# Two-layer graph network with a node update behind it: x + h and its moments formed in the second update, and one power and one row load per tile in the last stage

## What is computed

```python
h = jnp.maximum(_layernorm(x, axis=-1), 0.0)
x = x + _L0_gnn_ref(h, edge_index, ...)       # 2 attention layers, each followed by a node update
h = jnp.maximum(_layernorm(x, axis=-1), 0.0)
x = x + _L1_gnn_ref(h, edge_index, edge_attr_128, ...)

# inside the layers of _L0_gnn_ref, after the attention sum agg:
h = h + agg.reshape(n, TD) @ wo[l] + bo[l]
xn2 = _layernorm(h, ln2_g[l], ln2_b[l])
h = h + jax.nn.gelu(xn2 @ w1[l] + b1[l], approximate=False) @ w2[l] + b2[l]

# inside _L1_gnn_ref:
sum3d = jax.ops.segment_sum(edge_attr @ W_sum + b_sum, src)
cent_term = jax.nn.sigmoid(centralities @ W_cent + b_cent)
vor_term = jax.nn.sigmoid(voronoi_values @ W_vor + b_vor)
return h + z_in[in_deg] + z_out[out_deg] + cent_term + vor_term + sum3d
```

## Time and profile before

| what | value |
| --- | --- |
| median of 3 runs | 4993.78 us (4986.67 to 4995.4) |
| the profiled execution, its own time | 4956.99 us |
| span of its trace | 4955.3 us |
| busy share of the span: PE, DVE, ACT, POOL | 77%, 74%, 45%, 67% |
| second update, first power on POOL to last | 4150.2 to 4722.0 us of the span |
| last stage, first DVE instruction to the end | 4745.75 to 4955.3 us of the span |
| mean granted clock of TensorE | 0.911 |

### The profile page before, as it was taken

One profiled execution on the slowest core, in us unless ns is written; L12 is line 12 of the kernel. 1 busy time (PEld: TensorE's weight loads), 2 busy tenths in 40 slices (PEclk: granted clock), 3 DMA queues, 4 the chain that ended last, 5 costly groups with the idle time before them and its releaser, 6 DMA issues. The chain is left out here.

```text
span 4955.3 us, 83612 instructions
## 1 busy us (share of the span) xinstructions
PE 3801.7 (77%) x17590; PEld 2921.6 (59%) x17591; DVE 3657.7 (74%) x9953; ACT 2240.1 (45%) x5559; POOL 3311.4 (67%) x2905
## 2 busy tenths in 40 slices
PE   3686677777777777999986677777777776888879
PEld 1344455555555556888853455555555556778756
DVE  5686688888878886666655688888888886555568
ACT  0122465555556553444411466555555553333322
POOL 2266666666666654888877666666666654888857
PEclk9699899989999998999998899888999998999989
DMA  4577666666666655777766666666666655666668
GB/s 107 177 172 173 196 188 184 186 182 183 180 181 187 179 146 135 158 154 159 152 139 133 199 187 185 183 184 184 184 180 186 178 153 117 135 133 136 130 174 231
DMA packets 683596, 831.56 MB, mean 168 GB/s; under 512 B 147269, under 2 KB 524033, under 8 KB 683301
## 3 DMA queue, kind: packets, MB, share of 16 engines
q0 software_dynamic: 261248, 480.06, 40.0%
q1 hardware_dynamic: 389195, 320.33, 22.3%
q10 hardware_dynamic: 32860, 28.05, 1.9%
HBM read 753.54 MB, written 124.16 MB: 177 GB/s over the span
## 5 line engine op out<-in xcount | busy, mean ns | idle before, releaser
L1042 POOL DMA_INDIRECT kv<-kv_scratch,src_u x1760 | 1775.8, 1009 | 927.0 <-issue 540.1
L1308 PE MATMUL sum_p<-msg,hot_s 128*128 128x273 f32 x3520 | 1128.7, 460 | 541.2 <-DVE sums L1174 383.1
L1308 PEld LDWEIGHTS sum_p<-msg,hot_s 128*128 128x128 f32 x3520 | 704.7, 214 | 850.6 <-DVE sums L1174 396.1
L1514 POOL DMA_INDIRECT sum_scratch<-ysum,dest x600 | 952.6, 1588 | 192.5 <-issue 143.3
L1296 PE MATMUL qe<-sums,hot_q 128*128 x3520 | 909.3, 404 | 99.4 <-ACT hot_q L1064 85.5
L1296 PEld LDWEIGHTS qe<-sums,hot_q 128*128 128x128 f32 x3520 | 718.9, 207 | 245.4 <-issue 117.2
L1174 DVE SCALAR_TENSOR_TENSOR sums<-sums,keep,sum_p 128x273 f32 x880 | 433.8, 493 | 435.5 <-remote 352.0
L1073 ACT ACTIVATE hot_s<-iota_f,ndrel_u 128x128 f32<-128x128 f32 x1760 | 558.4, 391 | 169.2 <-remote 129.9
L1148 DVE TENSOR_TENSOR prod<-qe,kv 128x1024 f32<-128x1024 f32 x440 | 535.6, 1217 | 62.2 <-issue 20.9
L1163 DVE TENSOR_TENSOR msg<-kv,turned 128x1024 f32<-128x1024 f32 x440 | 532.7, 1211 | 6.4 <-issue 6.4
L1155 DVE TENSOR_REDUCE S<-prod 128x32 f32<-128x1024 f32 x440 | 533.9, 1213 | 0.6
(11 more groups left out here) (267 smaller groups left out, 5189.9 us busy)
## 6 DMA issues: line engine op xcount, KB each, us to landing
drow<-drel_scratch SPq DMA_DIRECT2D x220, 256.0 KB
kv<-kv_scratch,src_u POOLq DMA_INDIRECT x1760
ea<-in_edge_attr SPq DMA_DIRECT2D x52, 512.0 KB
srow<-in_src_rows SPq DMA_DIRECT2D x52, 512.0 KB
kv_scratch<-res SPq DMA_DIRECT2D x100, 256.0 KB
ea<-in_edge_attr SPq DMA_DIRECT2D x52, 384.0 KB
srow<-in_src_rows SPq DMA_DIRECT2D x52, 384.0 KB
hin<-h_scratch SPq DMA_DIRECT2D x154, 128.0 KB
```

The source lines that it names most:

```text
L1042: g.indirect_dma_start(out=kv[:, slot, :], out_offset=None, in_=KVd, in_offset=bass.IndirectOffsetOnAxis(ap=src_u[:, par, u:u + 1], axis=0 ...
L1308: ins = pe.matmul(sum_p[i][:, 0:XW], hot_s[:, q % 2, 2 * i + u, :], msg[:, q % 2, 2 * i + u, :], start=(u == 0), stop=(u == 1))
L1514: g.indirect_dma_start(out=sum_d[r], out_offset=bass.IndirectOffsetOnAxis(ap=dest[:, k, j:j + 1], axis=0), in_=ysum[:, k, j, :], in_offset ...
```

## The change

The second update also loads the tile's rows of x (`load_nodes`, behind a new wait), forms hx = h1 + x on DVE (`with_x`), adds the last product to hx in place of h1, so that x1 and no longer h is stored in `h_scratch`, and takes the moments of it. The last stage loads that x1 straight into its tile, loads no x, forms no sum and no moments, and takes one power over 128x50 at its start. The two sigmoids are added on DVE (sg_sum) and reach PSUM with one product instead of two, behind the gathered rows instead of ahead of them. The ones are written into the small tile `vec`, and SP's first load waits for nothing.

```diff
@@ update: SP
                             sp.dma_start(vin[:, k, :], rows(KVd, t * 2 + k)[:, D:2 * D]).then_inc(hv_in[k], 16)
+                            if last:
+                                sp.wait_ge(hx_s[k], t)
+                                sp.dma_start(xin[:, k, :], rows(x, t * 2 + k)).then_inc(x_in[k], 16)
@@ update: DVE
+                        def with_x(t, k):
+                            if last:
+                                v.wait_ge(h1_s[k], t + 1)
+                                v.wait_ge(x_in[k], t * 16 + 16)
+                                v.tensor_tensor(out=hx[:, k, :], in0=h1[:, k, :], in1=xin[:, k, :],
+                                                op=ALU.add).then_inc(hx_s[k], 1)
+
@@
-                            v.tensor_tensor(out=res[:, k, :], in0=w2_p[:, k * D:(k + 1) * D], in1=h1[:, k, :],
+                            if last:
+                                v.wait_ge(hx_s[k], t + 1)
+                            v.tensor_tensor(out=res[:, k, :], in0=w2_p[:, k * D:(k + 1) * D], in1=(hx if last else h1)[:, k, :],
                                             op=ALU.add).then_inc(out_s[k], 1)
 
                         def next_moments(t, k):
-                            if held is None:
-                                return
@@ finish: SP
-                        sp.wait_ge(ones_s, 1)
@@
-                            sp.wait_ge(x1_s[k], t)
-                            sp.dma_start(xin[:, k, :], x_n).then_inc(n_in[k], 16)
-                            sp.dma_start(hin[:, k, :], h_n).then_inc(n_in[k], 16)
+                            sp.wait_ge(o_s[k], t)
+                            sp.dma_start(x1[:, k, :], x1_n).then_inc(n_in[k], 16)
@@ finish: POOL
-                            g.wait_ge(ve_s[k], t + 1)
-                            g.tensor_tensor(out=rs[:, k, :], in0=veps[:, k, :], in1=neghalf[:, :], op=ALU.pow).then_inc(rs_s[k], 1)
-
+
+                        g.wait_ge(var_s, 1)
+                        g.tensor_tensor(out=scales[:, 0:NT], in0=scales[:, 0:NT], in1=neghalf.to_broadcast([P, NT]),
+                                        op=ALU.pow).then_inc(scales_s, 1)
@@ finish: DVE
-                        v.memset(vecs[:, :, :], 1.0).then_inc(ones_s, 1)
+                        v.tensor_scalar(out=scales[:, 0:NT], in0=moments[:, 0:NT, 1], scalar1=EPS, scalar2=None,
+                                        op0=ALU.add).then_inc(var_s, 1)
+                        v.memset(vec[:, :, :, :], 1.0).then_inc(ones_s, 1)
@@
                         v.wait_ge(w_in_s, 16 * 8)
+                        v.wait_ge(scales_s, 1)
@@ finish: PE
-                            pe.wait_ge(sga_s[k], t + 1)
-                            for j in range(2):
-                                pe.matmul(s_p[k % 2][:, 0:D], ident[:, :], sg[:, k, j * D:(j + 1) * D], start=False, stop=False)
                             pe.wait_ge(zi_s[k], t * 32 + 32)
                             pe.matmul(s_p[k % 2][:, 0:D], ident[:, :], zi[:, k, :], start=False, stop=False)
-                            pe.matmul(s_p[k % 2][:, 0:D], ident[:, :], zo[:, k, :], start=False, stop=True).then_inc(sp_s[k], 1)
+                            pe.matmul(s_p[k % 2][:, 0:D], ident[:, :], zo[:, k, :], start=False, stop=False)
+                            pe.wait_ge(sgs_s[k], t + 1)
+                            pe.matmul(s_p[k % 2][:, 0:D], ident[:, :], sg_sum[:, k, :], start=False, stop=True).then_inc(sp_s[k], 1)
```

More of the change, by code:

```diff
@@ L1373, in update @@
                 vin = sb(ph, "vin", [P, 2, D])
+                last = l == L - 1
+                xin = sb(ph, "xin", [P, 2, D]) if last else None
+                hx = sb(ph, "hx", [P, 2, D]) if last else None
                 h1 = sb(ph, "h1", [P, 2, D])
@@ L1661, in _ @@
                         norm(0, 0)
+                        with_x(0, 0)
                         def turn(t):
@@ L1665, in turn @@
                             norm(t, 1)
+                            with_x(t, 1)
                             repeats(t + 1, 0)
@@ L1679, in _ @@
                         norm(PAIRS - 1, 1)
+                        with_x(PAIRS - 1, 1)
                         for k in range(2):
@@ L1850, in finish @@
                 sg = sb(ph, "sg", [P, FB, 2 * D])
-                st = sb(ph, "st", [P, FB, 6])
-                mv = sb(ph, "mv", [P, FB, 2])
-                veps = sb(ph, "veps", [P, FB, 1])
-                rs = sb(ph, "rs", [P, FB, 1])
+                sg_sum = sb(ph, "sg_sum", [P, FB, D])
                 xn = sb(ph, "xn", [P, FB, D])
@@ L1860, in finish @@
                 s = Names(pool)
-                w_in_s, ones_s, pool_go, aggr_go = s.many(4)
-                n_in, s_in, x1_s, st_s, mv_s, ve_s, rs_s, deg_s, tot_s = (s.many(FB) for _ in range(9))
+                w_in_s, ones_s, pool_go, var_s, scales_s = s.many(5)
+                n_in, s_in, sgs_s, deg_s, tot_s = (s.many(FB) for _ in range(5))
                 tt_s, tc_s, sp_s, sgm_s, sga_s, o_c, o_s, stored, p_c, vec_s = (s.many(FB) for _ in range(10))
@@ L1903, in load @@
                             sum_n = [rows(sum_d[r], n) for r in range(TABLES)]
-                            x_n, h_n = rows(x, n), rows(Hd, n)
+                            x1_n = rows(Hd, n)
                             sp.wait_ge(p_c[k], t)
@@ L1941, in start @@
                             v.tensor_tensor(out=tot[:, k, :], in0=pair[:, k, 0, :], in1=pair[:, k, 1, :], op=ALU.add).then_inc(tot_s[k], 1)
-                            v.wait_ge(n_in[k], t * 32 + 32)
-                            v.tensor_tensor(out=x1[:, k, :], in0=xin[:, k, :], in1=hin[:, k, :], op=ALU.add).then_inc(x1_s[k], 1)
                             v.wait_ge(tot_s[k], t + 1)
@@ L1946, in start @@
                                             scalar2=None, op0=ALU.min).then_inc(deg_s[k], 1)
-                            v.wait_ge(x1_s[k], t + 1)
-                            v.bn_stats(out=st[:, k, :], in_=x1[:, k, :]).then_inc(st_s[k], 1)
-                            v.wait_ge(st_s[k], t + 1)
-                            v.sem_inc(aggr_go, 1)
-                            v.bn_aggr(out=mv[:, k, :], in_=st[:, k, :]).then_inc(mv_s[k], 1)
-                            v.wait_ge(mv_s[k], t + 1)
-                            v.tensor_scalar(out=veps[:, k, :], in0=mv[:, k, 1:2], scalar1=EPS, scalar2=None,
-                                            op0=ALU.add).then_inc(ve_s[k], 1)
-                        def total(t, k):
-                            c = t * 3
-                            v.wait_ge(rs_s[k], t + 1)
-                            v.tensor_scalar(out=xn[:, k, :], in0=x1[:, k, :], scalar1=mv[:, k, 0:1], scalar2=rs[:, k, :],
+                        def total(t, k):
+                            c, n = t * 3, t * FB + k
+                            v.wait_ge(sga_s[k], t + 1)
+                            v.wait_ge(sp_s[k], t)
+                            v.tensor_tensor(out=sg_sum[:, k, :], in0=sg[:, k, 0:D], in1=sg[:, k, D:2 * D], op=ALU.add).then_inc(sgs_s[k], 1)
+                            v.wait_ge(n_in[k], t * 16 + 16)
+                            v.tensor_scalar(out=xn[:, k, :], in0=x1[:, k, :],
+                                            scalar1=moments[:, bass.ds(n, 1), 0:1].rearrange("p n c -> p (n c)"),
+                                            scalar2=scales[:, bass.ds(n, 1)],
                                             op0=ALU.subtract, op1=ALU.mult).then_inc(o_c[k], 1)
-                            v.wait_ge(sp_s[k], t + 1)
                             v.wait_ge(stored[k], t * 16)
-                            v.scalar_tensor_tensor(out=acc[:, k, 0, :], in0=bsum_b[:, :], scalar=tot[:, k, ED:ED + 1],
-                                                   in1=s_p[k % 2][:, 0:D], op0=ALU.mult, op1=ALU.add).then_inc(o_c[k], 1)
                             v.wait_ge(o_c[k], c + 1)
@@ L1967, in total @@
                                                    op0=ALU.max, op1=ALU.add).then_inc(o_c[k], 1)
+                            v.wait_ge(sp_s[k], t + 1)
+                            v.scalar_tensor_tensor(out=acc[:, k, 0, :], in0=bsum_b[:, :], scalar=tot[:, k, ED:ED + 1],
+                                                   in1=s_p[k % 2][:, 0:D], op0=ALU.mult, op1=ALU.add).then_inc(o_c[k], 1)
                             v.wait_ge(o_c[k], c + 3)
```

11 lines of the change are left out of this document (7 added, 4 removed).

## The result

The change makes the kernel faster by about 0.4%: 4969.98 us (median of 5 runs, 4965.53 to 4976.92) against 4993.32 us of the kernel before on the same chip, ratio 0.9961 (95% interval 0.9949 to 0.9972). That is 23.3 us less; the forecast was 29.

What follows compares the result with a forecast made beforehand. Prediction: DVE and PE tie as the last stage's bound, 3.5 us a tile. Second update 0 + start 9.4 + slots 19.6 = 29 us, so 4993.8 - 29 = 4964.8 us; 8-in-10 range 4948 to 4985.

Steps and rivals of the forecast that it cites:

- The second update costs 0: Second update: 1.2 us a tile added on DVE hides in its idle time; cost 0, bounds 0 and 60 us.
- The port rival: Second update: POOL stands still during each hx on DVE, 0.42 us each, 21 us in all, 4986 us; chance 0.03.
- The scatters wait for landings: Second update: POOL's scatters wait for late landings; at 0.8 us a tile the kernel takes 5005 us; chance 0.07.
- The start, 9.4 us: Last stage's start: memset of 10.72 us gone, first pair then waits for one 8.35 us power; gain 9.4 us.
- The slot term, 3.55 to 3.15: Last stage: each slot shrinks from 3.55 to 3.15 us, saving 0.40 us, over 49 slots 19.6 us.
- Round this loop: Last stage: loop of sg_sum, PE's product, acc and back through DVE takes 3.0 us, just under PE's own 3.05.
- 0.03 for waits that don't fit exactly: Last stage's slot: 0.03 us allowed for mismatched waits, on top of PE's 3.05 and the loop's 0.07 us.
- PE's 3.05: Last stage: PE loses one 0.43 us product per tile and goes from 3.48 to 3.05 us.
- DVE 2.85 us, at most 3.2: Last stage: DVE's slot falls from 3.50 to 2.63 us, plus 0.2 for dependent pairs: 2.85, at most 3.2.
- DMA limits from below at 3.05: Last stage: without x a tile moves 776 KB instead of 904; at share 0.92 the slot is no less than 3.05 us.
- if the clock stays at 2.4 GHz: Last stage's start: PE's clock stays up, giving 6 us; with 2.9 us slots 47 us in all, 4946 us; chance 0.12.
- The changed kernel's profile, forecast at 4928 us: Whole kernel: profiled execution, 4956.99 us before, should take 4928 us; the runs' median lies 36.8 us above the profile.

Runs made afterwards that it cites:

- kernel 2: Changed kernel's second update in front of the old last stage, which adds x a second time: ratio 0.9997 to the kernel before, -1.5 us.
- Kernel 1: Kernel before with only the ones written into the small tile vec and SP's first load waiting for nothing: ratio 0.9968, -16.2 us.
- kernel 9: Changed kernel with total and attributes three tiles behind, x1's load later, sg_sum one slot ahead of its acc: ratio 0.9913 to the kernel before, -38.7 us.
- kernel 4: Kernel before with sg_sum alone: sigmoids added on DVE, one PE product less, the acc reading PE's sum moved behind the other: ratio 1.0091, +42.3 us.
- kernel 7: Changed kernel with filler, PE products of unused result, at the last stage's start and behind its first two begins: ratio 0.9944 to the kernel before, -23.7 us.
- kernels 3: Changed kernel without sg_sum, both sigmoids reaching PSUM with two PE products as before: ratio 0.9968 to the kernel before, -17.9 us.
- 5: Changed kernel with the power of the first 48 tiles taken on POOL at the second update's end: ratio 0.9959 to the kernel before, -17.7 us.
- 6: Changed kernel with SP's load of x1 issued one slot later, behind the next tile's sin: ratio 0.9959 to the kernel before, -16.5 us.
- 10: Changed kernel with lag of three tiles, sg_sum one slot ahead, and unused PE products at the last stage's start: ratio 0.9917 to the kernel before, -39.7 us.
- 12: Changed kernel with sg_sum taken one slot ahead, the lag staying at two tiles: ratio 0.9957 to the kernel before, -18.9 us.
- kernel 8: Changed kernel with total and attributes three tiles behind instead of two, x1's load two slots later: ratio 0.9944 to the kernel before, -26.7 us.

## Why the prediction was right, and where its sizes were off

- *The second update costs 0*: right, by kernel 2 (-1.5 us, interval -5.5 to +3.0) and by which waits shrank. The port rival, 21 us for 50 additions hx, is thereby excluded for these scatters: the powers are 571.3 us from first to last, as before (571.8). The exclusion in the Trainium skill, "SBUF — State Buffer", section "SBUF: two separate sides", is against a GpSimd operation that reads SBUF; against these indirect DMAs it didn't show.
- *The scatters wait for landings*: one wait of 0.8 us behind the last power, and 0.3 at most up to it. The rival didn't happen.
- *The start, 9.4 us*: 9.3 measured, by the mechanism named. Kernel 1 adds that without the power the loads would hold the first pair until 6.83 us, so the power costs 1.9 us there.
- *The slot term, 3.55 to 3.15, was mis-sized*: 3.55 to 3.34 by the same profile row, 3.28 from tile 12 on in the second profile. Two steps carry that. The step "Round this loop", 3.0 us, took in sg_sum, product and acc but not the gathers, whose loop takes 9.87 us for three slots. And "0.03 for waits that don't fit exactly" was far too little for two loops and one engine that all take between 3.0 and 3.3 us, and for an acc that twice started 0.7 to 2.2 us after its product had ended. Of the 19.6 us some 9 to 10 came. With both loops loosened (kernel 9) the slot is 3.10: PE's 3.05 was right.
- *DVE 2.85 us, at most 3.2*: in kernel 4 one new dependent pair and the moved instructions cost 0.28 us, where I took 0.2 for the whole new order; DVE wasn't full in the changed kernel, so this isn't where the slots went.
- *DMA limits from below at 3.05*: kernel 9 holds 3.10 us at a share of 0.89 to 0.91, so the limit is as near as computed. The rule of the Trainium skill in "DMA: Bandwidth & Descriptors", section "Latency and other measured facts", that latency grows under load, may be in the 4.2 us of zo; no run here varied the load alone.
- *The clock* stood only among the upside rivals ("if the clock stays at 2.4 GHz"). The step "the gain is 9.4 us" took for granted that the clock would rise 9.4 us earlier as well. It rose as late as before, so more slots ran at 5.8 us, for 2.9 us in these profiles. PE's idle time ahead of the stage did shrink, from 28.5 to 15.1 us, and the clock was at its lower level after it all the same, so the rival "if the clock stays at 2.4 GHz" didn't come true. From one profile of the changed kernel to the next the rise moves by 5 us (35 and 30), and in the second one only 0.7 us are lost.
- *The median*: forecast 4965, measured 4970. By stages 9.3 + 9.2 - 2.9 + 0.9 = 16.5 us; the runs show 23.3 with an interval of 14 to 25, which holds that; the second profile's stage gives 19.8 us. That 4970 came so near 4965 is in part luck: by the stages 9 to 12 of the 29 us are missing, and the runs happen to lie 3.5 to 7 us above the stages. The changed kernel's profile, forecast at 4928 us, took 4969.98, because stages ahead of the change took 29.7 us longer in it, which no step of the prediction could know.

## What to carry to other kernels

When an engine that was full gets relief, write down every loop that goes through two or more engines and a transfer, divide its length by the slots that it spans, and put that beside the engine's own time; a loop within 10% of it is a bound too, as this one was (3.29 us to 3.05). A lag of one tile more costs only buffers that are already there, but it pays only if no other handover within the slot is as tight; test the cures together as well as alone. And look first at the plain work in front of a stage: here one memset brought 11.3 us by the profiles, and all the rest of the change 5 to 9.

## What the runs showed of the hardware

- PE's granted clock rose 18 to 35 us after the last stage's start in kernels without filler whose first product came at 6 to 7 us (with the small memset) and no later, 26 to 34 us, in the three that keep the large memset, where the first product came some 11 us later. With products from the very start (kernel 7) it rose after 3 us, and fell again behind five microseconds of which PE was busy 1.34. In kernel 4 its mean was 0.80 over 50 us in which PE was busy 44.7: there, work moved from PE to DVE cost clock.
- From the row numbers (ideg) to the start of the gather that needs them pass 0.98 to 1.04 us in every slot from tile 12 on, in ten profiles (the changed kernel twice, kernels 3, 5 to 10 and 12), whether POOL was idle or not. From the start of the second gather to PE's product it was 4.2 us in the slot shown, at a DMA share of 0.86, and 3.5 to 5.0 us in the second profile.
- In kernel 8 acc started 1.0 us after PE's product had ended by its row (4856.06 to 4857.11), several times, and in the changed kernel once by 2.24 us. No row says why; in kernel 9, with the lag of three and the sum ahead, the waits from 4400 to 4520 us have none. This stays open, and with it how much of the slots' loss in the changed kernel is the handover's.
